# Row sums of squares in a four-layer graph kernel: four transposes and one VectorE sum in place of four one-column products

## The reference, cut to what matters

```python
h = jax.nn.relu(hypergraph_conv(x, adj, W1, b1))   # [128, 128, 512]
h = layer_norm(h, gamma, beta)                      # mean and variance over the 512
y = hypergraph_conv(h, adj, W2, b2)
return y + x
```

## Time and profile before

| what | value |
|---|---|
| time, median of 3 runs | 1412.56 us (1412.31, 1412.56, 1417.0) |
| span of the profiled execution, first to last instruction | 1411.1 us |
| the profiled execution's own time | not given apart from the three runs; their median lies 1.5 us above the span |
| TensorE busy | 1367.8 us (97%) |
| VectorE busy | 1271.7 us (90%) |
| ScalarE busy | 1053.6 us (75%) |
| GpSimd busy | 946.2 us (67%) |
| mean granted TensorE clock | 0.990 of full speed |
| HBM traffic | 38 GB/s over the span |

### The profile page before, as it was taken

The page is one execution under the profiler, slowest core; times in us unless marked ns, Lnnn a source line. Parts: engine busy times, 40 slices in busy tenths (PEclk is TensorE's granted clock), DMA queues, the critical chain, the costliest instruction groups (busy, mean ns, idle before and its releaser), DMA issues.

```text
span 1411.1 us, 33599 instructions
## 1 busy us (share of the span) xinstructions
PE 1367.8 (97%) x8954; PEld 1249.5 (89%) x8954; DVE 1271.7 (90%) x5267; ACT 1053.6 (75%) x2345; POOL 946.2 (67%) x972
## 2 busy tenths in 40 slices
PE   7789999999999999999999999999999999999986
PEld 6678999999999999999999999999999999999975
DVE  6879999999999999999999999999999999999884
ACT  4557777877777887777887777787777788777764
POOL 5657766667766666766666776666786666676533
PEclk9899999999999999999999999999999999999999
DMA  4000111101111101111110111110111111111001
GB/s 127 31 31 23 39 39 54 54 23 45 52 39 50 52 29 43 47 52 37 52 47 27 45 52 37 52 52 22 45 52 45 44 52 35 39 45 37 31 31 53
DMA packets 75384, 62.16 MB, mean 44 GB/s; under 512 B 3013, under 2 KB 70985, under 8 KB 75338
## 3 DMA queue, kind: packets, MB, share of 16 engines
q1 hardware_dynamic: 75338, 61.63, 13.7%
HBM read 36.45 MB, written 16.78 MB: 38 GB/s over the span
## 4 chain that ended last, share of the span: by engine, by line
PE 92%; DVE 5%; issue 2%; ACT 1%; POOL 0%; DMA 0%; DVEq 0%; ACTq 0%; POOLq 0%
PE ps L371 39%; PE ps L356 25%; PE ps L375 20%; PE ps L477 4%; PE ps L432 3%; DVE stats L1590 1%; DVE prod L1774 1%; PE ps L633 0%; DVE h L1602 0%; DVE x L1737 0%; PE ps L629 0%; DVE x L1685 0%; DVE z L1730 0%; DMA adj_f<-in_adjT 0%; DVE el L1675 0%
## 5 line engine op out<-in xcount | busy, mean ns | idle before, releaser
L1315 POOL TENSOR_TENSOR x3n<-p,x 128x512 f32<-128x512 f32 x63 | 80.9, 1284 | 259.8 <-ACT p L982 259.8
L1275 POOL TENSOR_TENSOR hT_lo<-hT,hT_hi 128x512 fp32r<-128x512 f32 x126 | 161.3, 1302 | 57.0 <-ACT hT L924 42.1
L1255 POOL TENSOR_TENSOR rs<-var_e,neg_half 128x4 f32<-128x4 f32 x160 | 165.2, 1033 | 23.7
L903 ACT ACTIVATE p<-ps,rs 128x256 f32<-128x256 f32 (+1 forms) x256 | 136.6, 597 | 29.1 <-DVE sij L1691 28.8
L371 PE MATMUL ps<-wl_hi,h2T_hi 128*128 128x512 f32 (+1 forms) x512 | 149.1, 373 | 0.7 <-DVE x L1737 0.7
L356 PE MATMUL ps<-p,alT 128*128 128x256 f32 (+1 forms) x512 | 142.9, 382 | 0.5 <-DVE p L1715 0.5
L371 PE MATMUL ps<-wl_lo,h2T_hi 128*128 128x512 f32 (+1 forms) x512 | 132.8, 341 | 0.0
L375 PE MATMUL ps<-wl_hi,h2T_lo 128*128 128x512 f32 (+1 forms) x512 | 132.2, 340 | 0.0
L1590 DVE BATCH_NORM_STATS2 stats<-x 128x6 f32<-128x256 f32 x256 | 108.8, 425 | 5.7
L1000 ACT ACTIVATE h3T_hi<-ps 128x512 fp32r<-128x512 f32 x64 | 38.3, 598 | 91.0 <-PE ps L477 87.1
L924 ACT ACTIVATE hT_hi<-ps,cols_sb 128x512 fp32r<-128x512 f32 x128 | 87.4, 683 | 21.7 <-PE ps L375 21.5
(11 more groups left out here) (192 smaller groups left out, 4607.8 us busy)
## 6 DMA issues: line engine op xcount, KB each, us to landing
x_in<-in_x SPq DMA_DIRECT2D x32, 512.0 KB, 3.5
out_x<-x SPq DMA_DIRECT2D x32, 512.0 KB, 3.2
adj_f<-in_adjT SPq DMA_DIRECT2D x32, 256.0 KB, 2.8
adj_m<-in_adjT SPq DMA_DIRECT2D x32, 256.0 KB, 2.9
adj_l<-adj_m SPq DMA_DIRECT2D x32, 256.0 KB, 2.4
vqk<-in_l_wk SPq DMA_DIRECT2D x3, 256.0 KB, 4.6
x<-in_w1T SPq DMA_DIRECT2D x1, 512.0 KB, 6.7
x<-in_w2T SPq DMA_DIRECT2D x1, 512.0 KB, 7.7
```

The costliest lines, as they stand in the source:

```text
L903: return act.activation(dst, src, ACT.Copy, scale=scale)
L1255: pool.tensor_tensor(rs[:, layer, :], var_e[:, layer, :], neg_half[:], ALU.pow).then_inc(done, G)
L1275: pool.tensor_tensor(hTs[1][:, hc, :], hT[:, hc, :], hTs[0][:, hc, :], ALU.subtract).then_inc(S["hT_lo"], 1)
L1315: pool.tensor_tensor(x3n[:, s], p0[:, s], x2[:, s], ALU.add).then_inc(S["x3_ready"], 2)
```

## The change

The four one-column products become four transposes on TensorE: `sq[:, 0]` of a graph is turned so that its 128 nodes lie on the partitions and its 128 partial sums along the free axis, in columns `D + 4` to `D + 131` of the same PSUM bank. VectorE then sums the 128 columns of all four graphs in one `tensor_reduce` over the four banks, ahead of the copy of the mean. The factor 1/512 moves into the subtraction, which becomes a `scalar_tensor_tensor` and waits in addition for the new semaphore `hsq_ready`. Nothing is moved in any engine's list, and no transfer changes.

```diff
+    SQ = D + 4
...
+        hsq = sb("hsq", G)
...
             def front_sums(r, g):
                 pe.wait_ge(S["sq_done"], r.front(G))
-                product(bank("z", g)[:, D + 2:D + 3], lambda c: sq[:, 0, g * C:(g + 1) * C],
-                        lambda c: mean_w[:, 0:1], 1).then_inc(S["hsums_ready"], 1)
+                pe.transpose(bank("z", g)[:, SQ:SQ + P], sq[:, 0, g * C:(g + 1) * C],
+                             ident[:]).then_inc(S["hsums_ready"], 1)
...
+            def front_squares(r):
+                dve.wait_ge(S["hsums_ready"], r.front(G))
+                dve.tensor_reduce(hsq[:], four("z")[:, :, SQ:SQ + P], AX_X, ALU.add).then_inc(S["hsq_ready"], G)
+
             def front_variance(r):
-                dve.wait_ge(S["hsums_ready"], r.front(G))
+                front_squares(r)
                 dve.wait_ge(S["zr_ready"], r.front(G))
                 dve.tensor_copy(hst[:], four("z")[:, :, D]).then_inc(S["hst_ready"], G)
                 dve.wait_ge(S["hst_ready"], r.front(G))
                 dve.tensor_tensor(hmean[:, 0, :], four("z")[:, :, D], hst[:], ALU.mult).then_inc(S["hm_a"], G)
                 dve.wait_ge(S["hm_a"], r.front(G))
-                dve.tensor_tensor(hmean[:, 1, :], four("z")[:, :, D + 2], hmean[:, 0, :],
-                                  ALU.subtract).then_inc(S["hvar_ready"], G)
+                dve.wait_ge(S["hsq_ready"], r.front(G))
+                dve.scalar_tensor_tensor(hmean[:, 1, :], hsq[:], 1.0 / DH, hmean[:, 0, :], ALU.mult,
+                                         ALU.subtract).then_inc(S["hvar_ready"], G)
```

More of the change, by code:

```diff
@@ L214, in gnn_stack @@
         s_ready s_copied deg_a deg_b deg_ready rd_spread gt_ready nm0 nmr_ready res0_ready
-        yT_ready yT_copied yT_lo u_ready hT_ready hT_hi hT_lo sq_step sq_half sq_done hsums_ready zr_ready hst_ready hm_a hvar_ready vare_h rsh_ready z_ready
+        yT_ready yT_copied yT_lo u_ready hT_ready hT_hi hT_lo sq_step sq_half sq_done hsums_ready zr_ready hsq_ready hst_ready hm_a hvar_ready vare_h rsh_ready z_ready
         c2_ready x1_ready st1 ag1 nm1_ready h1_ready var1 rs1_ready
```

## The result

The changed kernel takes **1453.46 us** (median of 4, 1451.52 to 1454.95), the kernel before on the same chip 1412.43: ratio 1.028, 95% interval 1.026 to 1.030. The profiled execution of the changed kernel has its own time of 1454.95 us and a span of 1453.2, 42.1 more than before. The forecast was 1449.5, so the direction, the range and the rough size hold; 4 us are missing.

A forecast was written before the change was run, and what follows sets the result against it. The prediction took TensorE to bound the kernel: 28 rounds losing 1.28 us (35.8) plus 1.1 for the four others gave +36.9 on 1412.56, so 1449.5 us, 2.6% slower, range 1420 to 1457.

The forecast's parts named there:

- TensorE's saving, 0.35 us: On TensorE's chain, four transposes were to take 0.44 us where the four products took 0.79, 0.35 us less per round.
- The sum, 0.68 us and 0.60 of VectorE's list: On VectorE ahead of `hst`, the added sum was to take 0.68 us and lengthen the list by 0.60 (bounds 0.33, 0.82).
- `front_c2` waits some 0.25, `next_d` sets TensorE back by 0.36: TensorE waits 0.25 us for `z` at `front_c2`; at `next_d`, 0.24 us of slack leaves 0.36 of the 0.60 delay.
- the second rival: At `front_b1`, `wh` doesn't lose the port, so TensorE loses only 0.36 us at `next_d`: 1423.8 us, chance 0.20 including partial loss.
- `wh` loses the port in all rounds: `wh` meets GpSimd's `add_x4`, ends at 637.24, and `front_b1` starts 1.28 us later each round; chance 0.62 (nearly all rounds).
- the two rounds that the forecast leant on: Rounds 2 and 31 of the kernel before, where `wh` took 1.29 and 1.31 us, read as blocked by GpSimd.
- the fourth place: VectorE's waits for TensorE at `elu_low` and `mid_vb`: VectorE arrives 1.68 us later, TensorE 1.28, and the 0.40 difference fits.
- the 0.58 of room: VectorE's waits for TensorE per round near its end, 0.4 us ahead of `elu_low` and 0.2 ahead of `mid_vb`.
- the 36.9 forecast: Total predicted increase of the span in us: 28 rounds of 1.28 (35.8) plus 1.1 for the four other rounds.

## Why the prediction was right, and where it was short

What the forecast had for each place, and what came, as starts counted from the first of `front_sums`, in us, medians of the 27 rounds of index 3 to 29:

| start | before | changed | later by | forecast |
|---|---|---|---|---|
| TensorE, `mid_ap` of graph 0, behind `front_c2` | 11.75 | 11.93 | 0.18 | -0.10 |
| TensorE, `mid_ap` of graph 1, behind `next_d` | 12.62 | 12.91 | 0.29 | 0.36 |
| VectorE, `wh` | 13.34 | 13.87 | 0.53 | 0.60 |
| TensorE, `front_b1` | 14.12 | 15.32 | 1.20 | 1.28 |
| VectorE, `h3T_lo` | 14.09 | 15.69 | 1.60 | 1.68 |
| TensorE, `next_y`, behind `mid_ap` of graph 3 | 15.42 | 16.96 | 1.54 | 1.28 |

- **TensorE's saving, 0.35 us.** In the changed kernel's chain the four transposes take 0.45 us where the products took 0.79: right. Behind `front_c2` nothing of it is left on TensorE. Against the sum alone a round is 0.11 us shorter, and 0.21 where GpSimd waits in both.
- **The sum, 0.68 us and 0.60 of VectorE's list.** 687 ns, and 0.60 us in the chain. Right; the slope between two shapes of the same instruction was a good estimate. `wh` comes 0.53 us later.

```profile
640.12 0.45 PE ps L542 x4
...
641.18 0.60 DVE hsq L1722
```

- **`front_c2` waits some 0.25, `next_d` sets TensorE back by 0.36.** `front_c2` was taken too low: TensorE was to be 0.10 us early behind it and is 0.18 late. `next_d` waits for VectorE, so that the two don't add up: behind it TensorE is 0.29 late, a little less than forecast. With GpSimd's wait the changed kernel lost 0.40 us a round and took 1424.25 us; that the second rival, which has `next_d` alone, gave 1423.8 is in part luck: there TensorE is 0.28 us late at `front_b1`, and the wait of `mid_ap` of graph 3, which the rival doesn't have, brings it to 0.46.
- **`wh` loses the port in all rounds.** Shown: it did in rounds 3 to 30, for 1.29 to 1.32 us, it did with the sum alone and with the products alone made cheap, and the time went back when GpSimd waited. `centre_logits` follows `nmean` by 0.12 us in every one of these rounds, as forecast. Of the two rounds that the forecast leant on, round 2 has no `add_x4`: the GpSimd instruction that `wh` starts with there, in both kernels, is `add_res0` (at 132.20, for 1.27 us, in the kernel before). In round 31 of the changed kernel `wh` is recorded 0.02 us ahead of `add_x4` and took 0.17 us: it won the tie, the opposite of what that round showed before.
- **The step that failed: the fourth place.** I wrote that VectorE's further delay of 0.40 us fits into the 0.58 of room ahead of `elu_low` and `mid_vb`, so that a round loses 1.28 us. It lost 1.48. VectorE's waits there were not used up at all: 11.0 and 4.7 us over 27 rounds, against 11.1 and 4.7. Before VectorE comes to them it writes `h3T_lo`, 1.60 us later than before while TensorE is 1.20 to 1.22 later, and `mid_ap` of graph 3 waits for that. It is the 0.45 us in the waits above, a weight load's, of which TensorE's products lose 0.32; the chain of the changed kernel goes through it:

```profile
655.64 0.69 DVE h3T_lo L1486
656.38 1.59 PE ps L358 x10
```

So TensorE meets VectorE's delay once more, ahead of the place where I had put the room. What is missing is 0.20 us a round: 0.32 more at this place, 0.08 less at `front_b1`, and the last few hundredths come back later in the round. Over 28 rounds 0.20 is 5.6 us; the 36.9 forecast would have been 42.5, and the span grew by 42.1.

## What to carry to other kernels

Room that an engine shows late in a round is no cover for a delay earlier in it: walk its list from the delay to the room, and look at every semaphore that it raises on the way. Where two engines share a port, what counts is where their instructions fall in time; a change that only makes a third engine faster can bring them together, and it is cheap to order the two by a wait on the one that has time. A wait names the semaphore that rose last, which need not be the one that was needed: take the engine named off the suspect, or order the two, and see whether the wait goes.

## What the runs showed of the hardware that was not expected

- `wh` recorded 0.17 us before `add_x4`, while `add_bias` still runs, takes 0.23 us, so it gets in between the two (635.33, 635.50). Recorded within 0.01 us of `add_x4`, it lost in rounds 3 to 30 of the changed kernel, and with the cheap products in all but one of rounds 3 to 31. Recorded 0.02 us ahead, in round 31, it won in the changed kernel and lost with the short sum. So the recorded starts don't tell who wins a tie this close.
- The plain `tensor_scalar` on two elements per partition queued behind GpSimd four times in a row, 4.86 us, although it reads one tensor and one value per partition; the form with an accumulator didn't queue at all.
- Less work for TensorE alone, 0.45 us a round, made the kernel 1.8% slower.
